# A graph network's edge stage: the transposed one-hot compared from row lists that SP loads, instead of transposed on TensorE

## The chip, the cores and the metric

The kernel runs on one core of a Trainium2 chip. The metric is the device time of one execution in microseconds (us). The profile is of one execution; its span runs from the first instruction to the last. Five engines have instruction queues of their own: TensorE (PE), VectorE (DVE), ScalarE (ACT), GpSimd (POOL) and SyncE (SP, which here only issues transfers). DMA engines move data beside them.

## The reference, cut to what matters

A message-passing layer over 3125 nodes with 103,125 edges, then a node update and a feed-forward block on half of the nodes. The edge part is the larger one:

```python
hi = h[ei]                      # h: 3125 x 256, the layer-normed nodes
hj = h[ej]
x = jnp.concatenate((hi, hj, d2), axis=-1)
msg = jax.nn.silu(x @ mW1 + mb1)
msg = _layer_norm(msg, ln_g, ln_b)
msg = jax.nn.silu(msg @ mW2 + mb2)
agg = jax.ops.segment_sum(msg, ei, num_segments=h.shape[0])
y = jnp.concatenate((h, agg), axis=-1)
y = jax.nn.silu(y @ uW1 + ub1) @ uW2 + ub2
```

`ei` is a sorted list of nodes, `ej` the other end of each edge, `d2` one weight per edge.

## The kernel before

It has three blocks of code, each ended by a barrier over the engines.

**First block (0 to 423 us).** The product with mW1 is taken once per node and not per edge: `a_sb` holds `h @ mW1[0:256]` in SBUF, 25 blocks of 125 nodes, each as a high and a low part, and in partitions 125 to 127 below the nodes the weight row of `d2`; `b_table` holds `h @ mW1[256:512] + mb1` in DRAM. The edges are grouped by block of their node `ei` into 834 tiles of 128 edges (`TILES`), and one record per edge is scattered to `rec_d` in DRAM. A record has six planes (`PLANES`): 0 is the edge's node number in its block, plus one (zero for padding), 1 to 3 the weight `d2` split in three bf16 parts, 4 and 5 the number of node `ej` as two parts. At the end of the block SP loads the records back as `recT` (tile in the partition, L261, seven groups of up to 128 tiles), PE transposes each plane (L601), and ACT and DVE copy them in turn to `rec` (edge in the partition, L365 and L759).

**Second block, the edge stage (423 to 2013 us).** Its loop runs over 417 pairs of tiles (`PAIRS`), six pairs (`RING`) to an iteration of the hardware loop; the first 3 iterations (`PEEL`) and the last are written out. The code of each engine is one `slot(t, ...)` per pair, in which each step works on an older pair: `has(t, 3)` is the step for pair t - 3. The order inside a slot is written by hand, and semaphores tie the engines. The steps of one pair, with the slot in which each stands:

- DVE, slot t: `index` computes the gather indices of pair t + 2 (L1014), POOL gathers two tiles of rows of `b_table` to `g_rows` (L862) as soon as they are there.
- DVE, slot t: `ohb`, edge by node one-hot of both tiles (L1105: bf16 compare of `iota_n` with plane 0), and a copy of the three weight parts to columns 125 to 127 (L1107).
- slot t+1: PE transposes it to `psT` (L949), ACT copies `psT` to `ohT` (L906, two buffers).
- slot t+2: PE multiplies `ohT` with the block of `a_sb`, high and low part, two tiles: `psH` (L958, four products). DVE adds `psH` to `g_rows` (L1122).
- slots t+3 to t+9: ACT's silu to `act1` (L911), DVE's statistics of the rows (L1129), a rsqrt in 16 small DVE steps per three pairs (`newton`), ACT's normalization `normed` (L899).
- slots t+10 to t+14: PE transposes to `psM` (L976), ACT copies to `nT` (L920), PE multiplies with `w2g` to `ps2` (L984), ACT's silu to `msg` (L916), DVE's float32 one-hot `ohf` (L1114), PE's product `psG` that sums the edges per node (L967), DVE's two additions to `agg` (L1023).

PE's order in a slot is psT, psH, psG, psM, ps2. DVE's is agg, agg, ohb, its copy, idx_pair, ohf, g_rows, statistics, with rsqrt steps between them in two slots of three. In this stage SP loads six weights of the next block and then all of `x` to `x_sb` (L848, L849) and has nothing else to do; POOL clears `agg` after the sixth pair's gathers (L871), and after its last gather adds `h_sb` and a bias to `x_sb` (L882, L886).

**Third block (2013 us to the end).** Node update, feed-forward, ranking and output. The change leaves it as it is.

## Time and profile before

| | |
|---|---|
| three runs | 2300.64, 2305.55 and 7235.58 us, median 2305.55 |
| the profiled execution | 2300.03 us |
| its span | 2298.3 us |
| mean granted TensorE clock | 0.947 of 2.4 GHz |
| busy in the span: PE, DVE, ACT, POOL | 88%, 87%, 60%, 45% |

A row of the profile names a group of instructions by line, engine, operation, the tensors out<-in (buffer numbers left out) and shapes. A float32 product counts as two rows. The tile `ps` is `ps2`. A length is from an instruction's start to its end; successive instructions of one engine overlap by some of it, so what an instruction costs its engine is read from start to start. "Idle before" is time in which an engine had nothing running, with what released it; "issue" stands where the profile shows no releaser. PE's ends are modelled, its starts are better.

### The profile page before, as it was taken

The numbers are of one execution on the slowest core, as the hardware profiler recorded it, in microseconds if no ns is written. First come the engines' busy times: TensorE is split into PE (matmuls) and PEld (weight loads), VectorE is DVE, ScalarE is ACT, GpSimd is POOL, SyncE is SP. The second block draws the span as 40 slices with busy tenths as digits, with TensorE's granted clock in tenths as the row PEclk, the third lists the DMA queues.
The fourth block names the chain that finished last, engine by engine and source line by source line (L and its number), as shares of the span: only waits on it lengthen the run. The fifth ranks groups of instructions, "written<-read, shape, count | busy, mean of one in ns | idle before, by whom it ended". The sixth has DMA issues, their size and how long they took to land. (4 is left out here: it accounts for less than half of the span.)

```text
span 2298.3 us, 51635 instructions
## 1 busy us (share of the span) xinstructions
PE 2029.3 (88%) x11892; PEld 1711.3 (74%) x11893; DVE 1999.2 (87%) x6778; ACT 1385.4 (60%) x2909; POOL 1035.3 (45%) x1037
## 2 busy tenths in 40 slices
PE   3555764499999999999999999999999998799996
PEld 2324553388888888888888888888888886677775
DVE  6899999599999999999999999999999999736795
ACT  1112331388888888787777777777777776423331
POOL 8752222555555555555555555555555556203000
PEclk9987776599999999999999999999999999899998
DMA  3000000432222222222222222222222222010001
GB/s 122 0 1 24 25 25 17 147 94 71 73 71 73 69 73 72 70 73 71 71 73 69 72 71 71 73 71 71 73 71 71 71 70 59 1 40 1 28 1 56
DMA packets 65908, 135.17 MB, mean 59 GB/s; under 512 B 20973, under 2 KB 36451, under 8 KB 65606
## 3 DMA queue, kind: packets, MB, share of 16 engines
q0 software_dynamic: 42016, 111.40, 17.0%
q1 hardware_dynamic: 22577, 22.31, 3.1%
q10 hardware_dynamic: 1266, 0.83, 0.2%
q8 instruction: 27, 0.44, 0.1%
q14 instruction: 22, 0.18, 0.0%
HBM read 124.33 MB, written 10.16 MB: 59 GB/s over the span
## 5 line engine op out<-in xcount | busy, mean ns | idle before, releaser
L862 POOL DMA_INDIRECT g_rows<-b_table,idx_pair x834 | 790.4, 948 | 733.0 <-DVE idx_pair L1014 591.6
L984 PE MATMUL ps<-w2g,nT 128*128 128x256 f32 x3336 | 789.1, 379 | 0.0
L984 PEld LDWEIGHTS ps<-w2g,nT 128*128 128x128 f32 x3336 | 601.5, 190 | 64.5
L899 ACT ACTIVATE normed<-act,shift,rstd_e 128x255 f32<-128x255 f32 x834 | 453.8, 596 | 196.7 <-DVE shift L1086 196.2
L1023 DVE TENSOR_TENSOR agg<-psG,agg 125x256 f32 x834 | 348.4, 418 | 121.6 <-PE psG L967 41.5
L967 PE MATMUL psG<-msg,ohf 128*125 128x256 f32 x1668 | 430.1, 380 | 0.0
L1129 DVE BATCH_NORM_STATS2 stat_e<-act 128x6 f32<-128x256 f32 x834 | 313.8, 423 | 0.0
L958 PE MATMUL psH<-a_sb,ohT 128*128 x1668 | 304.4, 305 | 0.0
L920 ACT ACTIVATE nT<-psM 128x512 f32<-128x512 f32 x417 | 249.0, 597 | 90.1 <-PE psM L976 88.9
L967 PEld LDWEIGHTS psG<-msg,ohf 128*125 128x125 f32 x1668 | 283.9, 187 | 25.1 <-ACT msg L916 0.2
L1122 DVE TENSOR_TENSOR g_rows<-psH,g_rows 128x512 f32<-128x512 f32 x417 | 289.4, 694 | 11.5 <-DMA g_rows<-b_table,idx_pair 8.5
L911 ACT ACTIVATE act<-g_rows 128x512 f32<-128x512 f32 x417 | 260.4, 624 | 8.2 <-DVE g_rows L1122 8.0
L976 PE MATMUL psM<-identf,normed 128*128 128x128 f32 x1668 | 251.2, 273 | 0.0
L916 ACT ACTIVATE msg<-ps 128x512 f32<-128x512 f32 x417 | 246.4, 591 | 5.2 <-PE ps L984 5.2
L976 PEld LDWEIGHTS psM<-identf,normed 128*128 128x128 f32 x1668 | 209.1, 142 | 43.0 <-issue 0.2
L958 PEld LDWEIGHTS psH<-a_sb,ohT 128*128 128x128 f32 x1668 | 228.0, 193 | 0.9 <-issue 0.3
L906 ACT ACTIVATE ohT<-psT 128x256 fp32r<-128x256 bf16 x417 | 157.2, 377 | 79.8 <-PE psT L949 78.7
L1105 DVE TENSOR_TENSOR ohb<-iota_n,rec 128x250 bf16<-128x250 bf16 x417 | 175.7, 421 | 0.2 <-issue 0.2
L1114 DVE TENSOR_TENSOR ohf<-iota_n,rec 128x250 f32<-128x250 bf16 x417 | 173.5, 416 | 0.0
L949 PEld LDWEIGHTS psT<-identb,ohb 128*128 128x128 bf16 x834 | 81.1, 98 | 109.4 <-DVE ohb L1107 48.5
L949 PE MATMUL psT<-identb,ohb 128*128 128x128 bf16 x834 | 116.1, 221 | 48.4 <-DVE ohb L1107 39.7
L494 POOL DMA_INDIRECT rec_d<-recw,dest x62 | 59.8, 964 | 176.2 <-ACT recw L333 91.3
(201 smaller groups left out, 2406.1 us busy)
## 6 DMA issues: line engine op xcount, KB each, us to landing
g_rows<-b_table,idx_pair POOLq DMA_INDIRECT x834
h_sb<-in_x SPq DMA_DIRECT2D x1, 3125.0 KB
b_table<-b_out SPq DMA_DIRECT2D x25, 125.0 KB
x_all<-in_x SPq DMA_DIRECT2D x1, 3125.0 KB
out<-x_all SPq DMA_DIRECT2D x5, 625.0 KB
rec_d<-rec SPq DMA_DIRECT2D x1, 1668.0 KB, 8.7
agg<-rec_d SPq DMA_DIRECT2D x6, 256.0 KB, 4.2
row<-score_d SPq DMA_DIRECT2D x1, 1525.9 KB
```

Source lines behind the costliest of these rows:

```text
L862: pool.indirect_dma_start(g_rows[:, j, n, :], None, b_table[:, :], bass.IndirectOffsetOnAxis(ap=idx_pair[:, j, n:n + 1], axis=0)).then_inc ...
L899: ins = nc.scalar.activation(normed[:, (j - 9) % 2, n, 0:D - 1], act1[:, (j - 9) % RING, n, 0:D - 1], ACT.Identity, scale=rstd_e[:, 1 - fa ...
L911: nc.scalar.activation(act1[:, (j - 3) % RING, :, :], g_rows[:, (j - 3) % RING, :, :], ACT.Silu).then_inc(s_act1, 1)
L916: nc.scalar.activation(msg[:, j % 2, :, :], ps2[:, j % 2, :, :], ACT.Silu).then_inc(s_msg, 1)
L920: nc.scalar.activation(nT[:, j % 2, :, :, :], psM[:, :, :, :], ACT.Copy).then_inc(s_nT, 1)
L958: mm = pe.matmul(psH[:, j % 2, n, :], ohT[:, j % 2, n, :], rows, start=(part == 0), stop=(part == 1))
L967: mm = pe.matmul(psG[0:NB, k, n, :], ohf[:, k, n, :], msg[:, k, n, :], start=True, stop=True)
L976: mm = pe.transpose(psM[:, n, q, :], normed[:, j % 2, n, q * P:(q + 1) * P], identf[:, :])
L984: mm = pe.matmul(ps2[:, k, n, :], nT[:, k, n, q, :], w2g[:, q, :], start=(q == 0), stop=(q == 1))
L1023: V.tensor_tensor(room, psG[0:NB, j % 2, n, :], room, ALU.add).then_inc(s_agg, 1)
L1122: V.tensor_tensor(g_rows[:, k, :, :], psH[:, j % 2, :, :], g_rows[:, k, :, :], ALU.add).then_inc(s_hid, 1)
L1129: ins = V.bn_stats(stat[:, q // 3, 2 * (q % 3) + n, :, :].rearrange("p h w -> p (h w)"), act1[:, q, n, :])
```

## The change

The transposed one-hot (node in the partition, edge in the column) is no longer made by transposing `ohb`. It is compared directly, by one DVE instruction per pair: a row list of the 256 edges' node numbers, the same in all 125 partitions, against the partition's own number (`node_col`). SP loads the lists, three pairs at a time (a half ring), from the DRAM tensor `loc_d` to `loc_rows`, broadcast to 125 partitions; and in a second transfer the three weight parts from `ew_d` into partitions 125 to 127 of `ohT`, which now has six buffers. Both DRAM tensors are written at the end of the first block from `recT`, whose tile-in-partition form has the edges of a tile in a row already: DVE copies plane 0 to `loc_c`, ACT planes 1 to 3 to `ew_c` as float32, SP stores them. Only planes 0, 4 and 5 are still transposed into `rec`, all of them copied by DVE. `ohb`, `psT` and ACT's copy are gone. The float32 one-hot `ohf` compares against a float32 row `nodes` in PSUM in place of the bf16 `iota_n` in SBUF.

```diff
@@ first block, SP: after the seven loads of recT
+                for g in range(TG):
+                    n = min(P, TILES - g * P)
+                    sp.wait_ge(s_locc, g + 1)
+                    sp.dma_start(loc_d[g * P:g * P + n, :], loc_c[0:n, g, :]).then_inc(s_rows_out, 16)
+                    sp.wait_ge(s_ewc, g + 1)
+                    sp.dma_start(ew_d[g * P:g * P + n, :, :].rearrange("t n r -> t (n r)"),
+                                 ew_c[0:n, g, :, :].rearrange("t n r -> t (n r)")).then_inc(s_rows_out, 16)
+                sp.wait_ge(s_rows_out, 32 * TG)
...
@@ first block, ACT
-                for g in range(0, TG, 2):
+                for g in range(TG):
                     n = min(P, TILES - g * P)
-                    act.wait_ge(s_rx, g + 1)
-                    nc.scalar.activation(rec[:, g * P:g * P + n, 0:PLANES], psR[:, 0, :, 0:n].rearrange("p n t -> p t n"),
-                                         ACT.Copy).then_inc(s_rec[0], 1)
+                    act.wait_ge(s_recT[g], 16)
+                    nc.scalar.activation(ew_c[0:n, g, :, :], recT[0:n, g, :, 1:4].rearrange("t r n -> t n r"),
+                                         ACT.Copy).then_inc(s_ewc, 1)
...
@@ first block, PE
-                    for k in range(PLANES):
-                        mm = pe.transpose(psR[:, g % 2, k, 0:n], recT[0:n, g, :, k], identb[0:n, 0:n])
+                    for k, plane in enumerate((0, 4, 5)):
+                        mm = pe.transpose(psR[:, g % 2, k, 0:n], recT[0:n, g, :, plane], identb[0:n, 0:n])
...
@@ first block, DVE
-                for g in range(1, TG, 2):
+                for g in range(TG):
+                    n = min(P, TILES - g * P)
+                    dve.wait_ge(s_recT[g], 16)
+                    V.tensor_copy(loc_c[0:n, g, :], recT[0:n, g, :, 0]).then_inc(s_locc, 1)
+                for g in range(TG):
                     n = min(P, TILES - g * P)
                     dve.wait_ge(s_rx, g + 1)
-                    V.tensor_copy(rec[:, g * P:g * P + n, 0:PLANES],
-                                  psR[:, 1, :, 0:n].rearrange("p n t -> p t n")).then_inc(s_rec[1], 1)
+                    V.tensor_copy(rec[:, g * P:g * P + n, 0:3],
+                                  psR[:, g % 2, :, 0:n].rearrange("p n t -> p t n")).then_inc(s_rec, 1)
...
@@ edge stage, SP
+                def body(d):
+                    for h in range(2):
+                        first = d * RING + h * (RING // 2)
+                        if not has(first, 0):
+                            continue
+                        need(sp, s_first, first - RING // 2)
+                        own = bass.ds(2 * first, RING)
+                        sp.dma_start(loc_rows[:, h, :, :].rearrange("p t e -> p (t e)"),
+                                     loc_d[own, :].rearrange("(a t) e -> a (t e)", a=1).broadcast_to([NB, RING * P])).then_inc(
+                            s_loc_in[h], 16)
+                        sp.dma_start(ohT[NB:P, h * (RING // 2):(h + 1) * (RING // 2), :, :].bitcast(F32).rearrange(
+                            "k t n e -> k (t n) e"), ew_d[own, :, :].rearrange("t k e -> k t e")).then_inc(s_ew_in[h], 16)
+
+                filling(body)
                 for to, frm in todo:
                     sp.dma_start(to, frm, allow_slow_non_contiguous=True).then_inc(s_late, 16)
                 sp.dma_start(x_sb[:, :, :], x_v).then_inc(s_xin, 16)
+                with sp.Fori(PEEL, DG) as d:
+                    body(d)
+                draining(body)
...
@@ edge stage, ACT
-                    if has(t, 1):
-                        act.wait_ge(s_turned, t)
-                        need(act, s_first, t - 2)
-                        nc.scalar.activation(ohT[:, (j - 1) % 2, :, :], psT[:, :, :],
-                                             ACT.Copy).then_inc(s_ohT, 1)
...
@@ edge stage, PE
-                    if has(t, 1):
-                        pe.wait_ge(s_oh, t)
-                        need(pe, s_ohT, t - 1)
-                        for n in range(2):
-                            mm = pe.transpose(psT[:, n, :], ohb[:, (j - 1) % RING, n, :], identb[:, :])
-                        mm.then_inc(s_turned, 1)
                     if has(t, 2):
+                        k = (j - 2) % RING
+                        if k % 3 == 0:
+                            pe.wait_ge(s_ew_in[k // 3], 16 * (d + 1 if j >= 2 else d))
                         pe.wait_ge(s_ohT, t - 1)
...
-                                mm = pe.matmul(psH[:, j % 2, n, :], ohT[:, j % 2, n, :], rows,
+                                mm = pe.matmul(psH[:, j % 2, n, :], ohT[:, k, n, :], rows,
...
@@ edge stage, DVE
-                    if has(t, 0):
-                        need(dve, s_turned, t - RING + 1)
-                        own = bass.ds(2 * t, 2)
-                        V.tensor_tensor(ohb[:, j, :, 0:NB], iota_n[:, 1:NB + 1].unsqueeze(1).broadcast_to([P, 2, NB]),
-                                        rec[:, own, 0].unsqueeze(2).broadcast_to([P, 2, NB]), ALU.is_equal)
-                        V.tensor_copy(ohb[:, j, :, NB:P], rec[:, own, 1:4]).then_inc(s_oh, 1)
+                    if has(t, 1):
+                        k = (j - 1) % RING
+                        if k % 3 == 0:
+                            dve.wait_ge(s_loc_in[k // 3], 16 * (d + 1 if j >= 1 else d))
+                        need(dve, s_first, t - RING)
+                        V.tensor_scalar(ohT[0:NB, k, :, :].rearrange("p n e -> p (n e)"), loc_rows[:, k // 3, k % 3, :],
+                                        node_col[0:NB, 0:1], None, ALU.is_equal).then_inc(s_ohT, 1)
...
-                        V.tensor_tensor(ohf[:, j % 2, :, :], iota_n[:, 1:NB + 1].unsqueeze(1).broadcast_to([P, 2, NB]),
+                        V.tensor_tensor(ohf[:, j % 2, :, :], nodes[:, :].unsqueeze(1).broadcast_to([P, 2, NB]),
```

How the instructions stand at three places. SP in the edge stage of before, from its first transfer to its last (`uw` are the next block's weights):

```order
L848 DMA uw<-in_L_gnn_uW 128x4x256
L848 DMA uw<-in_L_gnn_uW 128x2x256
L848 DMA ub1c<-in_L_gnn_ub 128x2x1
L848 DMA ub2b<-in_L_gnn_ub 128x256
L848 DMA wrb<-in_L_ffn_wr 128x256
L848 DMA brb<-in_L_ffn_br 128x1
L849 DMA x_all<-in_x 125x25x256
```

SP in the edge stage of the change, from the weights' load of the last of the six half rings that are written out to the first of the loop:

```order
L880 DMA ohT<-ew_d 3x6x128
L885 DMA uw<-in_L_gnn_uW 128x4x256
L885 DMA uw<-in_L_gnn_uW 128x2x256
L885 DMA ub1c<-in_L_gnn_ub 128x2x1
L885 DMA ub2b<-in_L_gnn_ub 128x256
L885 DMA wrb<-in_L_ffn_wr 128x256
L885 DMA brb<-in_L_ffn_br 128x1
L886 DMA x_all<-in_x 125x25x256
L887 UNCONDITIONAL_BRANCH
L887 ISA
L877 ISA [waits s_first]
L877 DMA loc_rows<-loc_d 125x768
```

The load of `x` has moved behind four waits on the loop's progress (`s_first`, before the third to the sixth half ring) and stands now in front of the loads of all later half rings.

PE inside the loop, one slot of before (ISA rows set an address register; a product of `x4` is four):

```order
L949 MATMUL psT<-identb,ohb 128x128 x2
L955 ISA
L958 MATMUL psH<-a_sb,ohT 128x256
L958 ISA
L958 MATMUL psH<-a_sb,ohT 128x256
L955 ISA
L958 MATMUL psH<-a_sb,ohT 128x256
L958 ISA
L958 MATMUL psH<-a_sb,ohT 128x256
L967 MATMUL psG<-msg,ohf 125x256 x2
L976 MATMUL psM<-identf,normed 128x128 x4
L984 MATMUL ps<-w2g,nT 128x256 x4
```

and one slot of the change:

```order
L987 ISA
L990 MATMUL psH<-a_sb,ohT 128x256
L990 ISA
L990 MATMUL psH<-a_sb,ohT 128x256
L987 ISA
L990 MATMUL psH<-a_sb,ohT 128x256
L990 ISA
L990 MATMUL psH<-a_sb,ohT 128x256
L999 MATMUL psG<-msg,ohf 125x256 x2
L1008 MATMUL psM<-identf,normed 128x128 x4
L1016 MATMUL ps<-w2g,nT 128x256 x4
```

The two transposes are gone and nothing else has moved, so psH follows ps2 of the slot before it directly.

DVE inside the loop, from the second agg addition of a slot, before:

```order
L1023 TENSOR_TENSOR agg<-psG,agg 125x256
L1040 TENSOR_TENSOR tmp<-stat_e 128x6
L821 REGISTER_ALU
L1105 ISA [waits s_turned]
L1105 TENSOR_TENSOR ohb<-iota_n,rec 128x2x125
L1107 ISA
L1107 COPY ohb<-rec 128x2x3
L1042 TENSOR_TENSOR tmp<-stat_e 128x6
```

and in the change, in a slot that begins a half ring:

```order
L1055 TENSOR_TENSOR agg<-psG,agg 125x256
L1072 TENSOR_TENSOR tmp<-stat_e 128x6
L1137 ISA
L843 REGISTER_ALU [waits s_loc_in0]
L1139 TENSOR_SCALAR ohT<-loc_rows,node_col 125x256 [waits s_first]
L1074 TENSOR_TENSOR tmp<-stat_e 128x6
```

One instruction stands where two stood. Before it wrote the one-hot of pair t, for PE's next slot; now it writes that of pair t - 1, also for PE's next slot.

## Rows read from the trace of the kernel before

**Rows 1.** the page, section 1: busy time, share of the span, instructions, by engine

```profile
PE 2029.3 (88%) x11892; PEld 1711.3 (74%) x11893; DVE 1999.2 (87%) x6778; ACT 1385.4 (60%) x2909; POOL 1035.3 (45%) x1037
```

**Rows 2.** stretches, mid-loop: length, busy us and instructions by engine, granted clock, DMA share, GB/s

```profile
600.00:1900.00 1300.00, 1300.00 (x7795) 1137.10 (x7794) 1196.61 (x5069) 1020.10 (x2126) 670.31 (x708) 1.00 0.25 71
```

**Rows 3.** PE in order of time, one slot: start us, length us, engine, line, operation, count

```profile
1200.27 0.27 PE L949 MATMUL psT<-identb,ohb 128*128 128x128 bf16 x2
...
1202.20 1.89 PE L984 MATMUL ps<-w2g,nT 128*128 128x256 f32 x8
...
1203.93 0.28 PE L949 MATMUL psT<-identb,ohb 128*128 128x128 bf16 x2
...
1204.02 0.71 PE L958 MATMUL psH<-a_sb,ohT 128*128 x4
...
1204.57 1.03 PE L967 MATMUL psG<-msg,ohf 128*125 128x256 f32 x4
```

**Rows 4.** DVE in order of time, mid-loop; in brackets idle before it and its releaser

```profile
1200.39 0.41 DVE L1023 TENSOR_TENSOR agg<-psG,agg 125x256 f32 x1
...
1204.15 0.41 DVE L1023 TENSOR_TENSOR agg<-psG,agg 125x256 f32 x1
...
1205.12 0.41 DVE L1105 TENSOR_TENSOR ohb<-iota_n,rec 128x250 bf16<-128x250 bf16 x1
1205.45 0.17 DVE L1107 COPY ohb<-rec 128x6 bf16 x1
1205.52 0.15 DVE L1069 TENSOR_TENSOR tmp<-tmp 128x6 f32<-128x6 f32 x1
...
1209.03 0.99 DVE L1023 TENSOR_TENSOR agg<-psG,agg 125x256 f32 x2 [1.06 <-issue]
```

**Rows 5.** PE in order of time, in the drain

```profile
1976.19 1.03 PE L967 MATMUL psG<-msg,ohf 128*125 128x256 f32 x4
...
1979.04 0.82 PE L958 MATMUL psH<-a_sb,ohT 128*128 x4
1979.69 1.03 PE L967 MATMUL psG<-msg,ohf 128*125 128x256 f32 x4
...
1982.72 1.03 PE L967 MATMUL psG<-msg,ohf 128*125 128x256 f32 x4
```

**Rows 6.** groups by line before 440 us: shapes, count, busy us and mean ns, idle

```profile
L749 DVE TENSOR_SCALAR w2g<-w2raw,gcol 128x256 f32<-128x256 f32 x2 | 0.6, 344 | 0.0
```

**Rows 7.** SP's issues in order of time: start us, length us, DMA, count

```profile
2.54 0.32 SPq L243 DMA_DIRECT2D h_sb<-in_x  x1
2.90 25.96 SPq L244 DMA_DIRECT2D wij<-in_L_gnn_mW  x1
...
426.45 0.34 SPq L849 DMA_DIRECT2D x_all<-in_x  x1
```

**Rows 8.** stretches, while h_sb is loaded; columns as in rows 2

```profile
12.00:16.00 4.00, 0.00 (x0) 0.00 (x0) 3.78 (x9) 0.00 (x0) 0.48 (x1) 1.00 0.34 121
```

**Rows 9.** DMA issues: queue, operation, count, KB each, median us to landing

```profile
rec_d<-rec SPq DMA_DIRECT2D x1, 1668.0 KB, 8.7
...
wrb<-in_L_ffn_wr SPq DMA_DIRECT2D x1, 128.0 KB, 4.9
```

**Rows 10.** waits of SP's queue: line, waited for, us in total, times, longest

```profile
SPq L851 <- DMA x_all<-in_x: 41.5, 1, 41.5
```

**Rows 11.** PE in order of time, after the idle time in the drain

```profile
1970.00 0.39 PE L949 MATMUL psT<-identb,ohb 128*128 128x128 bf16 x2 [27.68 <-DVE ohb L1107]
...
1971.23 1.91 PE L967 MATMUL psG<-msg,ohf 128*125 128x256 f32 x4
```

**Rows 12.** all engines in order of time, around the start of the edge stage

```profile
413.47 3.15 SPq L261 DMA_DIRECT2D agg<-rec_d  x7
...
433.51 0.69 DVE L1122 TENSOR_TENSOR g_rows<-psH,g_rows 128x512 f32<-128x512 f32 x1 [8.31 <-DMA g_rows<-b_table,idx_pair]
```

**Rows 13.** one line of the kernel, L1107: ns min/median/max, first and last start

```profile
L1107 DVE COPY ohb<-rec x417: 157/165/5952, 424.0 to 1973.4; 128x6 bf16 x132, 128x6 bf16<-128x6 bf16 x7
```

More of the change, by code:

```diff
@@ L94, in build @@
         rec = alloc(edge_mem, "rec", [P, TILES + 2 * LEAD, 8], BF16)
+        node_col = alloc(edge_mem, "node_col", [P, 1], F32)
         tile_block = alloc(edge_mem, "tile_block", [1, TG * P], I32)
@@ L228, in build @@
             s_rx = sem("s_rx")
-            s_rec = [sem("s_rec0"), sem("s_rec1")]
+            s_locc = sem("s_locc")
+            s_ewc = sem("s_ewc")
+            s_rows_out = sem("s_rows_out")
+            s_rec = sem("s_rec")
             s_tb = sem("s_tb")
@@ L769, in build @@
             idx_pair = sb("idx_pair", [P, RING, 2], I32)
-            ohb = sb("ohb", [P, RING, 2, P], BF16)
-            ohT = sb("ohT", [P, 2, 2, P], F32R)
+            loc_rows = sb("loc_rows", [NB, 2, RING // 2, 2 * P], BF16)
+            ohT = sb("ohT", [P, RING, 2, P], F32R)
             ohf = sb("ohf", [P, 2, 2, NB], F32)
@@ L781, in build @@
             shift = sb("shift", [P, 2, 6], F32)
-            psT = ctx.enter_context(nc.psum_tensor("psT", [P, 2, P], BF16))
+            nodes = ctx.enter_context(nc.psum_tensor("nodes", [P, NB], F32))
             psH = ctx.enter_context(nc.psum_tensor("psH", [P, 2, 2, D], F32))
@@ L794, in build @@
             s_gather = [sem(f"s_gather{j}") for j in range(RING)]
-            s_ohw = sem("s_ohw")
-            s_oh = sem("s_oh")
-            s_turned = sem("s_turned")
+            s_loc_in = [sem("s_loc_in0"), sem("s_loc_in1")]
+            s_ew_in = [sem("s_ew_in0"), sem("s_ew_in1")]
+            s_nodes = sem("s_nodes")
             s_ohT = sem("s_ohT")
@@ L990, in body @@
                     for j in range(RING):
-                        slot(d * RING + j, j)
+                        slot(d * RING + j, d, j)
                 filling(body)
@@ L1013, in index @@
                     own = bass.ds(2 * t, 2)
-                    V.scalar_tensor_tensor(out=idx_pair[:, j, :], in0=rec[:, own, 4], scalar=64.0, in1=rec[:, own, 5],
+                    V.scalar_tensor_tensor(out=idx_pair[:, j, :], in0=rec[:, own, 1], scalar=64.0, in1=rec[:, own, 2],
                                            op0=ALU.mult, op1=ALU.add).then_inc(s_idx, 1)
@@ L1140, in _ @@
                     index(t, t)
+                V.tensor_copy(nodes[:, :], iota_n[:, 1:NB + 1]).then_inc(s_nodes, 1)
+                dve.wait_ge(s_nodes, 1)
                 filling(body)
```

12 lines of the change are left out of this document (9 added, 3 removed).

## The prediction

> **What bounds the kernel now.** I read the page's first section first: TensorE (PE) is busy 88% of the span and VectorE (DVE) 87%, ScalarE (ACT) 60%, GpSimd (POOL) 45% [rows 1]. Two engines that close need the stage itself. The table of stretches shows from 600 to 1900 us, inside the edge loop, PE busy for all 1300 of 1300 us at a granted clock of 1.00 (2.4 GHz), DVE for 1197 and the DMA engines for a quarter [rows 2]. So I read one slot of the loop (one pair of tiles) in order of time on PE: the first psT product starts at 1200.27 and the next slot's at 1203.93, so a slot is 3.66 us [rows 3]. The loop from 456 to 1940 us holds about (1940 - 456) / 3.67 = 404 such full slots of the 417; the others are filling and draining.
>
> Does DVE bind as well? Its slots begin with an agg addition: two slots with rsqrt steps in them take some 3.76 us each (1200.39 to 1204.15), and before the third DVE stands idle for 1.06 us [rows 4]. So it needs about 3.67 - 1.06 / 3 = 3.32 us per slot. It has 0.35 us of slack, and PE sets the pace. POOL issues two gathers a slot and has about half of the slot free.
>
> **The change, part by part.**
>
> *PE loses the two transposes into psT (404 slots).* In a full slot psT starts 0.09 us before psH (1203.93 to 1204.02) and psH 0.55 us before psG, together 0.64 us [rows 3]. The smaller bound is therefore 0.09 us a slot. The larger one stands in the drain: exactly one slot there has psH and no psT. Its psG follows the previous psG after 1979.69 - 1976.19 = 3.50 us; the next slot, with neither, takes 1982.72 - 1979.69 = 3.03 us [rows 5]. So psH alone costs 0.47 us and psT plus psH 0.64: without psT a slot is 3.50 us, 0.17 less. That psH gets cheaper too is plausible, since its first weight load then stands behind a 0.21 us ps product (eight from 1202.20 to 1203.93) instead of behind a short transpose. I take 3.50, since it is the very sequence of the changed kernel at full clock, though it is one slot only. Gain: 404 x 0.17 = 69 us; with 0.09 it is 36.
>
> *ACT loses the copy of psT to ohT.* It is not the bound; nothing.
>
> *DVE loses ohb and its 6-column copy, and gains one tensor_scalar of 125x256 from bf16 in SBUF to ohT.* Start to start the old two take 0.33 + 0.07 = 0.40 us [rows 4]. The trace has no such operation on bf16; the nearest is w2g, 128x256 with a scalar per partition, 344 ns [rows 6]. The old pieces of 250 columns last 412 ns and cost 0.33, so the new one costs 0.27 to 0.33. DVE goes from 3.32 to about 3.2 us, under 3.50. The ohf compare reads its node numbers from PSUM now; agg, which reads PSUM too, lasts 0.41 us as ohb does [rows 4], so nothing. If PE's cover were gone DVE would still be 0.07 to 0.13 us quicker than before.
>
> *The order of the dependences.* Pair t is compared in DVE's slot t+1 and multiplied in PE's slot t+2, as the ACT copy was. DVE's compare lies early in a slot, two thirds of a slot or more ahead of the next psH. Its new waits: s_loc_in every third slot, and s_first of six pairs ago, which is long past. PE's new one is s_ew_in every third slot. Behind a late s_loc_in stands all of DVE's slot: the next index (so the gathers), the g_rows addition and the statistics.
>
> *SP loads 139 half rings of lists*, 125 partitions x 1536 bytes (188 KB) plus 9 KB of weights, each when the third pair before it is multiplied: that is 3 slots plus about one us before DVE needs it, some 11 us. Bounds of its time: h_sb, also 125 partitions, moved 3125 KB from 2.54 us to 28.86 at 121 GB/s, at which 188 KB take 1.6 us plus the fixed part [rows 7, 8]; the 128-partition broadcast wrb, 128 KB, landed in 4.9 us beside other loads [rows 9]. So 3.5 to 7 us against 11: hidden. The traffic is 188 KB per 10.5 us, 18 GB/s beside 71 for the gathers.
> The Trainium skill (DMA: Bandwidth & Descriptors, section "Why a DMA increments its semaphore by 16 and not by 1") says that the slowest dimension picks how many of the 16 engines a transfer uses, 5 for 125 partitions. The trace agrees: h_sb alone kept a share of 0.34 busy [rows 8].
>
> *SP's order moves the load of x (3125 KB).* It was issued at 426.45, at the head of the stage [rows 7], and no engine but SP waited for it until the loop's end. Now it stands behind six half rings and six weight loads, and in front of the list for pair 18. The sixth half ring (pairs 15 to 17) is let go when pair 11 is multiplied (PE slot 13); eight issues at about 0.45 us later, slot 14, x starts. DVE needs pair 18's list in slot 19, five slots or 18.5 us later. How long is x? 26.4 us nearly alone (h_sb) [rows 7], 41.5 us in the place it had, beside gathers (SP's own wait for it) [rows 10]. And does the list wait for it? The issue behind h_sb stood 25.96 us on SP, until h_sb was through [rows 7]; so yes. With x at 33 us, between the two because DVE's stall stops the gathers, plus 4.9 for the list: a stall of 33 + 4.9 - 18.5 = 19 us, bounds 13 and 28, and zero if the list's packets went beside x. After it PE restarts at the half clock: the slot after the idle 27.68 us in the drain has its psG at 1.91 us instead of 1.03 [rows 5, 11], so 2 us more. Sum +21, once.
>
> *Before the stage:* 14 more stores by SP behind the seven loads that took 3.15 us to issue, so 6.3 us of issues, overlapped with copies; 1.5 MB to store at the rate of rec_d (1668 KB in 8.7 us) is 8 us [rows 9, 12], starting as the first list lands. The rec copies now are all DVE's, seven of half the size. Most of it lies beside the transposes that ended the block before, so +3 us (0 to 8).
>
> *The stage's start:* the first gather was waited for until 433.51, 8.31 us, while x and the weights came in [rows 12]. Now only lists compete: -2 us (-4 to 0). POOL's clearing of agg blocks DVE as before, and POOL's additions to x after the last gather too.
>
> **Sum**, against the profiled execution (2300.03 us; the median of the runs shown, 2305.55, is 5 above): 2300 - 69 + 21 + 3 - 2 = 2253; I say 2255.
>
> **Rivals.**
> *A, the forecast: PE-bound at 3.50, x stalls the loop once.* 2255, own range 2235 to 2275. Chance 0.50, a little over half of it more than 2% under 2305.55 (below 2259).
> *B, no stall by x:* 2300 - 69 + 1 = 2232. For it: interleaving can't be ruled out, since h_sb's successor was a different transfer in a fuller queue. 0.12.
> *C, psT was worth only its 0.09 us:* 2300 - 36 + 22 = 2286. For it: only one slot shows 3.50. 0.14.
> *D, DVE's new operation meets GpSimd.* A copy of ohb stood 5.95 us while POOL cleared agg, and its median beside 50% gathers is 165 ns against a minimum of 157 [rows 13]. So gathers don't hold that 6-column copy. If they held the wider operation, it would meet one half of the time and wait half of 0.95 us, 0.25 us: DVE at 3.45 to 3.5, where every jitter shows; I price it at 3.58 a slot, 2300 - 36 + 22 = 2286 up to 2310. 0.10. The Trainium skill (SBUF — State Buffer, section "SBUF: two separate sides", its trap on DVE blocking DMA) says that a two-port DVE operation keeps GpSimd from writing descriptors; that would delay a gather by the operation's 0.3 us, out of a half-free slot.
> *E, slower: the lists come late each half ring.* It decides once a list needs more than the 11 us between its release and DVE's slot. Each us beyond that costs 139 us; at 13 us the kernel takes 2255 + 278 = 2530. Against it: 4.9 us for wrb. For it: the list's source is read 125 times from one row of DRAM, and no row shows that beside gathers. 0.08.
> Unnamed, anywhere: 0.06.
>
> About 2% is what a measurement of this kernel can tell from no change. Faster by over that: 0.28 of A, B, a little unnamed: 0.42. Slower: E, 0.02 of D, 0.02 unnamed: 0.12. Within: 0.46. The range goes from B to D's middle: 2228 to 2298.
>
> **What would show it.** PE's psG to psG in mid-loop: 3.50 (A, B), 3.58 (C, D). DVE's idle before agg: still about 0.9 us per three slots if PE leads, gone if D. One stall of 13 to 28 us on DVE near pair 18, some 490 us into the span, ended by the load of loc_rows, and x landing just before; none means B. DVE's waits for loc_rows each third slot mean E. The mean of the new tensor_scalar: 0.28 to 0.42 us long; more means D. First instruction of the edge stage at 425 to 431 us instead of 423.5. I am wrong if mid-loop slots are over 3.6 us, or if stall and prologue together exceed 35 us.

## The result and the profile after

The changed kernel takes 2271.84 us (median of four runs, 2270.75 to 2273.65), where the kernel before took 2304.62 in the same session (median of four, one of which took 7235.58). The ratio, which leaves that one run out, is 0.9865, with a 95% interval of 0.9848 to 0.9882. That is 1.35% faster, inside the 2% that I called "no change", 17 us above the 2255 I forecast and inside the range of 2228 to 2298. The profiled execution has a span of 2268.9 us against 2298.3. Its first section, to be read beside [rows 1]:

```profile
PE 1973.4 (87%) x11037; PEld 1678.5 (74%) x11038; DVE 1948.0 (86%) x6373; ACT 1295.1 (57%) x2495; POOL 1035.7 (46%) x1038
```

PE has 855 instructions fewer (834 of them the transposes into psT), DVE 405, ACT 414. A bare look at the shares says that nothing changed: two engines at 87% and 86%, as before. So I lined the two traces up by one event that both have, the start of DVE's addition `g_rows += psH` for pair p:

| pair | before, us | after, us | difference | what lies in between |
|---|---|---|---|---|
| 0 | 433.51 | 435.26 | +1.8 | prologue, first list, first gather |
| 15 | 478.98 | 482.20 | +3.2 | filling |
| 17 | 486.55 | 511.93 | +25.4 | the stall behind x: +22.2 |
| 30 | 534.54 | 558.32 | +23.8 | |
| 400 | 1894.32 | 1869.44 | -24.9 | 370 slots: -48.7, 3.675 to 3.544 us a slot |
| 416 | 1980.10 | 1953.54 | -26.6 | drain |
| end of span | 2298.3 | 2268.9 | -29.4 | the next block: -2.8 |

The last 2.8 us lie in a block that the change does not touch. PE's first row in it stands at 2013.2 us before and at 1986.9 after. Its first 15 us before, then after (columns as in [rows 2]; the clock is the third figure from the end), and PE's first 32 psU products in each:

```profile
2013.00:2028.00 15.00, 13.83 (x52) 9.92 (x53) 0.00 (x0) 4.42 (x8) 0.54 (x3) 0.77 0.49 150
2017.87 10.53 PE L1329 MATMUL psU<-fT,uw 128*128 128x320 f32 x32 [0.68 <-ACT fT L1270]
```

```profile
1986.64:2001.64 15.00, 13.38 (x68) 9.80 (x68) 0.00 (x0) 6.13 (x12) 0.54 (x3) 1.00 0.50 149
1990.83 8.68 PE L1364 MATMUL psU<-fT,uw 128*128 128x320 f32 x32 [0.68 <-ACT fT L1305]
```

The same 32 products take 10.53 us at a mean granted clock of 0.77 and 8.68 at 1.00; that is most of the 2.8 us, and luck as far as the change goes. From pair 416 to the end of the span the fourteen traces vary by 5.9 us (312.6 to 318.5).

The stall, on SP's queue and then on DVE, in order of time (start us, length us; in brackets the idle time before and what ended it):

```profile
467.84 0.26 SPq L877 DMA_DIRECT2D loc_rows<-loc_d  x1
...
472.76 0.37 SPq L886 DMA_DIRECT2D x_all<-in_x  x1
478.50 25.27 SPq L877 DMA_DIRECT2D loc_rows<-loc_d  x1
503.96 0.26 SPq L880 DMA_DIRECT2D ohT<-ew_d  x1
...
510.71 0.35 DVE L1139 TENSOR_SCALAR ohT<-loc_rows,node_col 125x256 fp32r<-125x256 bf16 x1 [22.34 <-DMA loc_rows<-loc_d]
```

The first issue behind x stands 25.27 us on SP. DVE waits 22.34 us for that list, and every engine is idle with it, as the stretches of the changed kernel show (columns as in [rows 2]):

```profile
500.00:510.00 10.00, 0.00 (x0) 0.00 (x0) 0.00 (x0) 0.00 (x0) 0.00 (x0) 0.50 0.34 121
510.00:520.00 10.00, 8.72 (x41) 7.68 (x41) 8.93 (x37) 4.43 (x9) 4.58 (x5) 0.76 0.21 63
600.00:1900.00 1300.00, 1300.00 (x7340) 1151.09 (x7339) 1191.07 (x4893) 976.01 (x1833) 695.84 (x734) 1.00 0.34 93
```

x moves at 121 GB/s with a DMA share of 0.34, the very figures of h_sb [rows 8]. By the Trainium skill (DMA: Bandwidth & Descriptors, section "Why a DMA increments its semaphore by 16 and not by 1") 125 partitions use 5 of 16 engines, a share of 0.31; the trace agrees, here as for h_sb. In mid-loop the DMA share is 0.34 instead of 0.25 and the traffic 93 GB/s instead of 71 [rows 2]: the lists are there, and nothing waits for them.

Now the slot. PE's psG products in mid-loop:

```profile
1203.99 1.03 PE L999 MATMUL psG<-msg,ohf 128*125 128x256 f32 x4
...
1207.49 1.02 PE L999 MATMUL psG<-msg,ohf 128*125 128x256 f32 x4
...
1211.11 1.12 PE L999 MATMUL psG<-msg,ohf 128*125 128x256 f32 x4
...
1214.71 1.02 PE L999 MATMUL psG<-msg,ohf 128*125 128x256 f32 x4
...
1218.21 1.03 PE L999 MATMUL psG<-msg,ohf 128*125 128x256 f32 x4
```

The distances between them are 3.50, 3.62, 3.60 and 3.50 us. Four of the six slots of a pass take the forecast's 3.50, two take 3.6, and the pass 21.26 us instead of 21.0. DVE in the same pass, in order of time:

```profile
1205.05 0.35 DVE L1139 TENSOR_SCALAR ohT<-loc_rows,node_col 125x256 fp32r<-125x256 bf16 x1
1205.31 0.16 DVE L1101 TENSOR_TENSOR tmp<-tmp 128x6 f32<-128x6 f32 x1
1205.42 0.16 DVE L1046 SCALAR_TENSOR_TENSOR idx_pair<-rec 128x2 int32 x1
...
1207.61 0.15 DVE L1118 SCALAR_TENSOR_TENSOR shift<-tmp,rstd_e 128x6 f32<-128x6 f32 x1
1208.86 0.99 DVE L1055 TENSOR_TENSOR agg<-psG,agg 125x256 f32 x2 [1.10 <-PE psG L999]
```

The new operation costs 0.26 us from start to start, just under the 0.27 to 0.33 that I had put. The 1.10 us of idle time is the point. The profile names PE's psG as its end, but psG of 1203.99 had long been done. In it stands work of DVE's own sequencer at the end of a pass of the loop: a branch and the load of twelve block numbers into registers. In the changed kernel, the times of that load (ns min/median/max, first and last start us):

```profile
L1042 DVEq TENSOR_LOAD <-tile_block x2: 851/851/851, 1207.6 to 1228.9; - x2
```

It comes every 21.3 us, once in six slots. In the kernel before the same load took 848 ns and began at 1207.8, inside the 1.06 us of [rows 4]. That branch and load fill the idle time is read from their place and length; no run took them out. What every trace shows is the 1.1 us itself, once a pass. The Trainium skill (DMA: Bandwidth & Descriptors, section "Latency and other measured facts") gives a floor of about 600 ns for such a load; here twelve registers took 851.

### The profile page after: what moved, and what is told of

Its sections match the earlier page's. It is cut to its first block and busy times, and to the rows that moved or that the text cites. A ratio compares the mean times of both kernels' runs of the same rounds, so it can differ in the third digit from the quotient of the medians.

```text
span 2268.9 us, 48446 instructions
## 1 busy us (share of the span) xinstructions
PE 1973.4 (87%) x11037; PEld 1678.5 (74%) x11038; DVE 1948.0 (86%) x6373; ACT 1295.1 (57%) x2495; POOL 1035.7 (46%) x1038
## 5 line engine op out<-in xcount | busy, mean ns | idle before, releaser
L999 PE MATMUL psG<-msg,ohf 128*125 128x256 f32 x1668 | 435.4, 383 | 0.0
L990 PE MATMUL psH<-a_sb,ohT 128*128 x1668 | 344.2, 329 | 67.6 <-issue 47.8
L990 PEld LDWEIGHTS psH<-a_sb,ohT 128*128 128x128 f32 x1668 | 258.6, 192 | 97.4 <-issue 76.1
L951 ACT ACTIVATE msg<-ps 128x512 f32<-128x512 f32 x417 | 241.5, 579 | 5.2 <-PE ps L1016 5.2
L1147 DVE TENSOR_TENSOR ohf<-nodes,rec 128x250 f32<-128x250 f32 x417 | 173.4, 416 | 0.0
L1139 DVE TENSOR_SCALAR ohT<-loc_rows,node_col 125x256 fp32r<-125x256 bf16 x417 | 150.3, 361 | 26.4 <-DMA loc_rows<-loc_d 26.1
L594 PE MATMUL psK<-oqv,or_ 128*128 128x96 bf16 x806 | 55.7, 232 | 80.6 <-DVE oqv L741 80.6
L349 ACT ACTIVATE recw<-psK 128x96 bf16<-128x96 f32 x62 | 15.4, 250 | 178.4 <-PE psK L594 151.8
L732 DVE TENSOR_TENSOR or_<-x_all,psV 128x1664 bf16<-128x1664 f32 x62 | 116.4, 1877 | 0.0
```

The source lines that it names most:

```text
L951: nc.scalar.activation(msg[:, j % 2, :, :], ps2[:, j % 2, :, :], ACT.Silu).then_inc(s_msg, 1)
L990: mm = pe.matmul(psH[:, j % 2, n, :], ohT[:, k, n, :], rows, start=(part == 0), stop=(part == 1))
L999: mm = pe.matmul(psG[0:NB, k, n, :], ohf[:, k, n, :], msg[:, k, n, :], start=True, stop=True)
```

## The experiments

Experiments 1 to 4 ran in one session, in which the kernel before took 2301.12 us. In the two sessions after it, it took 2316.37 and 2317.37, and in the last 2300.45. I call the first and the last calm and the two between them disturbed. It isn't the chip: one chip gave 2301, 2317 and 2300. Ratios are to the kernel before in the same session, and they do not take the session out: the same kernel has 0.9805 in a disturbed session and 0.9703 in a calm one (experiment 8), some 23 us apart. So times of experiments 5 to 7, all from disturbed sessions, are set against the changed kernel only to about that much; lengths in their traces are used where they can be.

What is different shows in the traces in mid-loop (600 to 1900 us). The disturbed ones have waits of ACT and DVE whose releaser the profile gives as "remote", together 48 to 347 us, and the calm ones have none. The same kernel in a disturbed session (engine and line, waited for, us in total, times, longest):

```profile
ACT msg L954 <- remote: 100.9, 78, 4.9
ACT nT L958 <- remote: 88.2, 35, 3.1
```

These waits come with loop passes of 24 to 26 us among normal ones, and the pipeline fills later (pair 15 at 489.8 us or later instead of 482 to 483).

**1. x in 25 pieces.** Is the stall the lists' place behind x?

```diff
-                sp.dma_start(x_sb[:, :, :], x_v).then_inc(s_xin, 16)
-                with sp.Fori(PEEL, DG) as d:
+                with sp.Fori(PEEL, PEEL + BLOCKS) as d:
+                    body(d)
+                    one = bass.ds(d - PEEL, 1)
+                    sp.dma_start(x_sb[:, one, :], x_v[:, one, :]).then_inc(s_xin, 16)
+                with sp.Fori(PEEL + BLOCKS, DG) as d:
                     body(d)
...
```

> The changed kernel with the one load of x taken apart: 25 pieces of 125 KB, one in each of the first 25 passes of SP's loop, behind the lists of that pass. Theory (the stall at 478 to 511 us is the lists standing behind x's 3.2 MB on one queue): at 121 GB/s a piece takes 1.1 us, which the 10.5 us between two half rings hide; the waits of SP (25.27 us) and of DVE (22.34 us) go, the clock does not fall to 0.5, and the time falls by 20 to 25 us, to 2247 to 2252, with a mid-loop slot of 3.54 as before. Rival 1 (the bandwidth that x takes, whatever its order, holds up lists and gathers): the same wait comes in pieces, most of the 20 us stays, 2262 to 2272. Rival 2 (the missing 17 us of the forecast came from x too, by a lasting effect on the pipeline's phase): the slot also falls to 3.50, 2230 to 2235.

Measured: 2248.43 us (ratio 0.9767, 0.9750 to 0.9783), 23.4 less than the changed kernel (22.6 by the ratios). Pair 17 starts at 490.42 instead of 511.93, and the mid-loop slot is 3.541 us: the first theory, and neither rival. SP's issues in order of time:

```profile
490.26 0.26 SPq L877 DMA_DIRECT2D loc_rows<-loc_d  x1
490.71 0.26 SPq L880 DMA_DIRECT2D ohT<-ew_d  x1
491.20 0.28 SPq L889 DMA_DIRECT2D x_all<-in_x  x1
500.75 0.26 SPq L877 DMA_DIRECT2D loc_rows<-loc_d  x1
```

No issue stands. The load of x costs nothing that the slot shows (3.541 against 3.544) when its pieces lie between two lists.

**2. x issued by ACT.** Order in one queue, or bandwidth?

```diff
+                        if isinstance(d, int) and d * RING + j == 13:
+                            act.dma_start(x_sb[:, :, :], x_v).then_inc(s_xin, 16)
```

> The changed kernel with the whole load of x issued by ACT at about the same time (behind ACT's slot 13, some 470 us) instead of by SP. Theory A (first in, first out: the lists wait only because they stand in SP's queue behind x): SP's wait at the list load goes, DVE's longest wait is under 3 us, and the time falls by 18 to 25 us, to 2247 to 2254. Theory B (the 16 DMA engines are shared, and x's traffic slows whatever else is loaded): the lists and the gathers land late for as long as x is moving, a stall of 10 us or more stays (at 187.5 KB a half ring, half the bandwidth would still bring a list in 3 us, so B needs more than fair sharing), 2260 to 2272.

Measured: 2249.36 us (0.9775, 0.9758 to 0.9791). The transfer is the same, whole and 2.6 us earlier, on another queue. ACT's queue and SP's in order of time, then the stretch:

```profile
470.17 0.29 ACTq L960 DMA_DIRECT2D x_all<-in_x  x1
...
479.51 0.30 SPq L877 DMA_DIRECT2D loc_rows<-loc_d  x1
```

```profile
500.00:510.00 10.00, 10.00 (x60) 8.92 (x58) 8.53 (x33) 7.64 (x15) 4.77 (x6) 1.00 0.50 165
```

The list's issue takes 0.30 us instead of 25.27 and the engines work on while 165 GB/s move. So the 22 us were the order in SP's queue, and the bandwidth of x was harmless.

**3. No compare for the second one-hot.** Who sets 3.544? The kernel leaves out DVE's compare in the loop, so its sums are not the reference's.

```diff
-                    if has(t, 12):
-                        V.tensor_tensor(ohf[:, j % 2, :, :], nodes[:, :]..., rec[:, ..., 0]..., ALU.is_equal).then_inc(s_ohf, 1)
```

> The changed kernel without DVE's compare for the second one-hot (ohf, 416 ns by its rows, some 0.33 us from start to start, once a slot): ohf is filled twice ahead of the loop and left, so the sums by node are not the reference's. PE's work is unchanged. Theory (DVE sets the slot in the changed kernel: 6 x 3.36 + 1.1 us at its loop's end = 21.26 us a pass, where PE needs 21.0): DVE's pass falls to 19.3 us, PE's 3.50 decides, the slot falls from 3.544 to 3.50, and the time by 15 to 19 us, to 2253 to 2257. Rival (PE's own loop end costs the 0.26 us a pass): slot 3.54, time within 3 us of 2272.

Measured: 2247.21 us (0.9768, 0.9752 to 0.9784), 24.6 less. The slot is 3.497 us, and all 62 mid-loop passes take 20.97 to 20.99. DVE is busy 1111 of 1300 us and now waits for PE's psH, which it does not in the changed kernel. The stretch, and the wait (engine and line, waited for, us in total, times, longest):

```profile
600.00:1900.00 1300.00, 1297.97 (x7424) 1161.45 (x7422) 1111.25 (x4562) 998.39 (x1857) 705.64 (x743) 1.00 0.34 94
```

```profile
DVE g_rows L1152 <- PE psH L990: 59.5, 146, 0.7
```

The two spans differ by 23.2 us: 17.1 lie in the 370 slots, as the theory has it; another 2.5 in pairs 17 to 30, 0.8 in the drain and 2.8 in the next block, which the edit doesn't touch. The expectation had counted the slots alone.

**4. The same cut in the kernel before.**

> The same cut in the kernel before: the compare that writes ohf is made twice ahead of the loop and left, so the sums by node are not the reference's. DVE's pass there is 22.05 us, PE's 22.0. Theory (PE set the slot before, DVE stood just under it): the slot stays 3.667 to 3.675, and the time falls by 0 to 4 us, 2300 to 2305. Rival (DVE set the slot before as well, and PE's rows of 3.667 are only DVE's pace): the slot falls by 0.02 us or more, the time by 8 us or more, to 2296 or less.

Measured: 2298.18 us (0.9986, 0.9976 to 0.9996), 2.9 less. PE in order of time:

```profile
1200.78 1.02 PE L968 MATMUL psG<-msg,ohf 128*125 128x256 f32 x4
1203.81 0.28 PE L949 MATMUL psT<-identb,ohb 128*128 128x128 bf16 x2
1204.44 1.02 PE L968 MATMUL psG<-msg,ohf 128*125 128x256 f32 x4
```

Every pass takes 22.00 us, against 22.05 in the kernel before. DVE waits for psH now, 177 times in mid-loop, so 22.00 us is what PE needs; the kernel before, in which DVE never waits for psH, takes the 22.05 that DVE needs. The two bounds lay 0.05 us apart. Experiments 3 and 4 take the same work from DVE; it is worth 17 us in the loop where PE needs 21.0, and 3 where it needs 22.0.

**5. Two transposes back on PE, of a constant, without a wait.** Their PSUM tile takes the place of `nodes`, so ohf compares against the bf16 row in SBUF again (417 ns; 416 in the kernel before).

```diff
+                        for n in range(2):
+                            pe.transpose(psT[:, n, :], iota_n[:, :], identb[:, :])
...
```

> The changed kernel with two transposes of 128x128 BF16 put back on PE in every slot, of a constant, into a PSUM tile that nobody reads and without a wait; the second one-hot is compared from the constant in SBUF again, as in the kernel before (416 ns either way by the rows). So DVE keeps its relief and PE loses its own. Theory (the two transposes cost PE 0.17 us a slot, and PE at 3.667 decides again): slot 3.66 to 3.68 against 3.544, 404 slots by 0.124 = +50 us, 2318 to 2326. Rival (the transposes slip into gaps of PE, and what the change gained was DVE's work and the round trip of the psT copy on ACT): slot under 3.60, 2272 to 2290.

Measured: ratio 1.0062 (1.0045 to 1.0079), 2330.31 us; by its ratio the changed kernel would take 0.9865 x 2316.37 = 2285 there, so +45, give or take what the session does. The trace doesn't depend on that. PE in order of time:

```profile
762.59 1.03 PE L1001 MATMUL psG<-msg,ohf 128*125 128x256 f32 x4
...
765.62 0.28 PE L982 MATMUL psT<-identb,iota_n 128*128 128x128 bf16 x2
...
766.26 1.03 PE L1001 MATMUL psG<-msg,ohf 128*125 128x256 f32 x4
```

psG follows psG after 3.66 or 3.67 us nearly everywhere in mid-loop, and the mean slot is 3.678. The transposes are worth 0.17 us of PE's slot, as the forecast had it, without any round trip through ACT. With them back, DVE's relief brings nothing, and what is left is the stall.

The trace also shows what DVE needs by itself. At 648.5 us a long pass had put 7.4 us between two g_rows of DVE, where 3.67 is normal; while DVE catches up, its passes are 21.31 and 21.25 us long and PE's 22.00. DVE, one row a pass, then PE:

```profile
677.20 0.69 DVE L1157 TENSOR_TENSOR g_rows<-psH,g_rows 128x512 f32<-128x512 f32 x1
...
698.51 0.69 DVE L1157 TENSOR_TENSOR g_rows<-psH,g_rows 128x512 f32<-128x512 f32 x1
...
719.76 0.68 DVE L1157 TENSOR_TENSOR g_rows<-psH,g_rows 128x512 f32<-128x512 f32 x1
```

```profile
678.26 1.03 PE L1001 MATMUL psG<-msg,ohf 128*125 128x256 f32 x4
...
700.26 1.03 PE L1001 MATMUL psG<-msg,ohf 128*125 128x256 f32 x4
```

DVE's own pass with the change is thus 21.25 us, the mid-loop pass of the changed kernel.

**6. Lists let go two pairs later.**

```diff
-                        need(sp, s_first, first - RING // 2)
+                        need(sp, s_first, first - RING // 2 + 2)
```

> The changed kernel with each half ring of lists released two pairs later (SP waits for psH of pair first-2 instead of first-4): the release then comes about 2.5 us ahead of the compare that needs the list, and the first list of the stage took 4.4 us from its issue (428.11) to the compare (432.54). Theory (lists are harmless only because of their lead, and every us that they are late costs once a half ring, since DVE sets the slot): late by 1.5 to 2.5 us in each of 139 half rings, +200 to +330 us, 2480 to 2600. Rival (in mid-loop a list lands in 2.5 us or less, or PE's lead takes it up): under +60 us.

Measured: 2305.40 us, ratio 0.9951 (0.9935 to 0.9967), 20 us above the changed kernel by ratio, which is within what the session alone can do, and far from the 200 and more that I expected. DVE waited for lists in mid-loop four times, together 4.4 us:

```profile
DVE ohT L1139 <- DMA loc_rows<-loc_d: 4.4, 4, 1.2
```

54 of 62 mid-loop passes take 21.2 to 21.4 us, as with the early lists. The extra is 9 us in the filling (pair 15 at 491.15 instead of 482.20) and five passes that last 24.4 to 26.1. Both belong to the session: the other kernels of the disturbed sessions have pair 15 at 489.8 to 495.7, with the lists let go early. So the later lists cost the 4.4 us of waits and nothing more that can be seen. My expectation took the landing time of the very first list, 4.4 us, for that of all. The forecast's rival E (lists late in every half ring) has about two slots of room: let go that much later, the lists only begin to be waited for.

**7. The indices off DVE.** If DVE sets the slot, taking its index operation away should bring PE's 3.50. All indices are made once, and ACT copies two a slot:

```diff
+                def index(t, j):
+                    nc.scalar.activation(idx_pair[:, j, :], idx_all[:, bass.ds(2 * t, 2)], ACT.Copy).then_inc(s_idx, 1)
...
+                    if has(t, 0):
+                        index(t + LEAD, (j + LEAD) % RING)
```

> The changed kernel with DVE's index operation (two elements, once a slot, about 0.1 us from start to start) taken from its loop: all indices are made in one DVE operation ahead of the loop, and ACT, which has idle time, copies two of them a slot into the ring. Theory (DVE sets the slot by 21.26 us a pass, PE needs 21.0): DVE's pass falls by some 0.5 us, PE's 3.50 decides, the slot falls from 3.544 to 3.50 and the time by 14 to 22 us, to 2250 to 2258, less 1 to 2 for the big operation. Rival 1 (ACT's new 0.2 us a slot lengthens its chain of waits to psM and normed): slot 3.54 or more. Rival 2 (the 24.6 us of the run without ohf came from its lighter load on PSUM or from the filling, not from DVE's share of the slot): under 10 us.

> Both edits on the changed kernel: x in 25 pieces, one a pass, and the indices copied by ACT. The two causes lie in different places (the stall at 478 to 511 us, the slot from 530 us on), so theory says that they add: 23.4 + 14 to 22 us, 2226 to 2235. Rival (the stall hid part of the filling's cost or the index copies on ACT eat the rest): 2238 or more, one of the two gains lost.

Measured: 2563.04 us, ratio 1.1048 (1.1026 to 1.1070), and with x split 2538.20, 1.0935 (1.0905 to 1.0965). The slot is 4.27 us. The x split kept its 25 us. The index edit went with some 280 us by the ratio, in a disturbed session; it was never run in a calm one. Two more kernels, both with x split, went after that. One has DVE make the indices of three pairs in one operation, once in three slots; one has ACT's copy at the head of its slot, about 1.8 us earlier:

> The changed kernel with x in 25 pieces and DVE's index operation made once in three slots for three pairs (6 elements), behind g_rows of the slot two ahead of the first of them, instead of once a slot for one. DVE's work falls by two operations of 0.08 to 0.1 us in three slots. Theory (DVE sets the slot, the gathers have lead enough): DVE's pass falls to under 21.0, PE's 21.0 decides, slot 3.50, 68 by 0.26 = -17 us, ratio to before 0.969 to 0.972. Rival (what made the kernel with ACT's index copies 10% slower is the gathers' release, three pairs in a bunch, and not ACT): here too POOL issues three pairs in a row after a wait, DVE waits for gathers in mid-loop, slot 3.6 to 4.3, ratio 0.99 to 1.09.

> The changed kernel with x in 25 pieces and the index copies on ACT, but at the head of ACT's slot, ahead of the two normed operations, instead of behind act1 (there the slot was 4.26 us). The index is then ready about 1.8 us earlier, ACT's work is the same. Theory A (the late release of the gathers was what cost 0.7 us a slot): the slot falls to 3.50 to 3.60, ratio to before 0.97 to 0.98. Theory B (the small operation on ACT itself disturbs: ACT's own chain to msg and nT, or something of that chip): slot 4.2 or more as before, ratio over 1.08.

Measured: 2591.73 us, ratio 1.1182 (1.1159 to 1.1205), slot 4.39, with ACT not involved; and 2314.17, ratio 0.9984 (0.9974 to 0.9994), slot 3.68, with ACT's copy early. So ACT's small operation is not needed for the loss. What the three slow ones share is that POOL waits up to 5 or 7 us for indices and then issues its gathers without a pause. From the kernel with three pairs at a time, POOL, then PE and ACT, in order of time:

```profile
1205.36 0.95 POOL L905 DMA_INDIRECT g_rows<-b_table,idx_pair  x1 [4.68 <-DVE idx_pair L1048]
1206.61 0.94 POOL L905 DMA_INDIRECT g_rows<-b_table,idx_pair  x1 [0.30 <-issue]
...
1211.62 0.95 POOL L905 DMA_INDIRECT g_rows<-b_table,idx_pair  x1 [0.30 <-issue]
```

```profile
1208.06 0.60 PE L1011 MATMUL psM<-identf,normed 128*128 128x128 f32 x4
...
1212.58 0.60 ACT L958 ACTIVATE nT<-psM 128x512 f32<-128x512 f32 x1 [5.01 <-remote]
```

Six gathers stand from 1205.36 to 1212.57. PE's psM ends at 1208.66, ACT's copy of it starts only at 1212.58, and DVE's next g_rows, for a psH that ended at 1210.85, at 1214.34. By counting the rows, the gather that this g_rows needs belongs to the bunch before, whose last issue was at 1199.74; in the three slow kernels every gather in mid-loop is issued 10.4 us or more before the g_rows that needs it, and in the changed kernel 9.9 or more. So the gathers are not late. Nor is a row of six enough: the six closest starts of a pass span 7.6 us in the changed kernel and 7.3, at one place 6.4, in experiment 3 (calm), and no pass of either is long; in the slow kernels it is 6.7 and 6.3. The rival is the session: all four kernels with changed indices ran in disturbed sessions, and the "remote" waits that end ACT's and DVE's idle time here are in every trace of those sessions and in no calm one. The session alone is not enough either: experiments 5 and 6 have slots of 3.68 and 3.60 us in it. Whether the index edits cost anything in a calm session is untested, and why ACT and DVE start 3.5 us or more after the PE rows that they need is open.

**8. One small DVE operation less.** This way to relieve DVE leaves the indices and gathers alone. The sum of the means and the sum of the moments become one operation over 12 elements, on top of the split x:

```diff
-                        V.tensor_tensor(mean2, m0, m1, ALU.add).then_inc(s_newton, 1)
...
-                        V.tensor_tensor(moment, q0, q1, ALU.add).then_inc(s_newton, 1)
+                        V.tensor_tensor(tmp[:, 1:3, :].rearrange("p w k -> p k w"), stat[:, par, :, 0, 1:3],
+                                        stat[:, par, :, 1, 1:3], ALU.add).then_inc(s_newton, 1)
...
```

> The changed kernel with x in 25 pieces (as before: 2248 where the kernel before took 2301, ratio 0.977) and one DVE operation less in each three slots: the sum of the two halves' means and the sum of their moments are made by one operation over 12 elements instead of two over 6. Theory (DVE sets the slot; its pass of 21.26 us falls by twice 0.08 us): pass 21.10, slot 3.517, 68 passes by 0.16 = -11 us, ratio to before 0.972 to 0.974. Rival 1 (what DVE saves is lost in its waits, or PE's loop end is the bound): pass 21.25, ratio 0.976 to 0.978. Rival 2 (the 12-element operation is slower by what is saved): the same.

> The same kernel as in the run of the merged sum (x in 25 pieces, one DVE operation less in three slots) once more. There, 50 or so of its 62 mid-loop passes took 21.0 to 21.4 us, and nine took 22.9 to 24.9, with ACT and DVE idle for 2 to 5 us behind PE's rows; the kernel before was itself 0.7% slower in that session than where the split was measured. Theory 1 (the long passes belong to the session, not to the kernel): where the kernel before takes 2301 us again, the long passes are gone, slot 3.51 to 3.52, 2236 to 2242, ratio 0.972 to 0.974; where it takes 2317 again, they are there again, ratio 0.980. Theory 2 (the faster DVE itself brings the long passes): they are there whatever the kernel before takes, ratio 0.979 to 0.982.

Measured first, in a session with the kernel before at 2317: ratio 0.9805 (0.9781 to 0.9829), 54 of 62 mid-loop passes at 21.0 to 21.44, seven of 22.9 to 24.9 (the nine of my expectation were a miscount). Measured again, with the kernel before at 2300: 2232.67 us, ratio 0.9703 (0.9690 to 0.9716), no long pass, slot 3.502. So the long passes belonged to the session, and they cost this kernel 41 us (2273.87 against 2232.67) where the kernel before lost 17. PE and DVE in order of time in the second run:

```profile
1202.67 1.03 PE L1002 MATMUL psG<-msg,ohf 128*125 128x256 f32 x4
...
1206.17 1.02 PE L1002 MATMUL psG<-msg,ohf 128*125 128x256 f32 x4
```

```profile
1203.46 0.17 DVE L1075 TENSOR_TENSOR tmp<-stat_e 128x12 f32<-128x12 f32 x1
```

The pass is 21.01 us, within 0.03 of what PE needs (20.99 in experiment 3). I had allowed 0.16 us for the two operations saved in a pass; 21.26 became 21.01, so they were worth 0.25. Why more is not shown. The rsqrt steps' starts lie 0.07 us before the next operation in some places and up to 0.22 in others. This kernel beats both: 3% under the kernel before, 1.6% under the changed one.

## Why the prediction was right or wrong

*PE's 0.17 us from the transposes: right.* It rested on one slot of the drain, which was indeed the sequence of the changed kernel: 3.50 in four of six slots (after), in all of them once DVE is out of the way (experiments 3 and 8), and 3.67 again with the transposes back (experiment 5). Rival C (0.09 us, 3.58 a slot) is out.

*"Before the third slot DVE stands idle for 1.06 us. So it needs 3.32 us per slot. It has 0.35 us of slack": wrong, and this is the step that failed.* The idle time was read once, in a window of 9 us, and spread over three slots. It comes once in six, and it is no slack: DVE has it in every pass, also when it lags behind PE, where its sequencer branches and loads registers. DVE needed 22.05 us a pass, that is 3.675 a slot, not 3.32. The trace of the kernel before could have told. These are all of DVE's waits of 600 to 1900 us in it:

```profile
DVE agg L1023 <- issue: 33.7, 32, 1.1
DVE agg L1023 <- PE psG L967: 28.5, 27, 1.1
```

Both are that one gap, 59 times in 59 passes. For psH, which it would wait for if PE led, DVE never waits. The sign that I had named, idle time before agg if PE leads, cannot tell the two: the gap of 1.1 us stands once a pass whoever leads (59 times in experiment 4, where PE does). With the right number the forecast's own prices give the result: DVE trades 0.33 + 0.07 for 0.27, 0.13 us a slot or 0.80 a pass, and 22.05 - 0.80 = 21.25 is above PE's 21.0. 404 slots by 0.133 are 54 us instead of 69, and 2300 - 54 + 21 + 3 - 2 = 2268, against 2270.75 us of the profiled execution and 2271.84 of the median. This one term is 15 of the 17 us.

*The stall, +21: right in place, cause and size.* Pairs 15 to 17 lost 22.2 us, DVE waited 22.34 until 510.71, and the issue behind x stood 25.27. By pair 30 the changed kernel is 21.5 us behind experiment 1, which has no stall. The parts were each off by 2 to 3 us and partly cancel: x held the queue for 31.0 us (33 expected), the list took 6.9 more (4.9), and DVE needed it 15.6 us after x started (18.5). The reading that an issue behind a long load stands until it is through, taken from h_sb [rows 7], held, and experiment 2 shows that it holds for one queue only. Rival B is out; it had the right time only for a kernel without the stall (experiment 1: 2248, and 2232 with DVE relieved too).

*The prologue, +3 (0 to 8), and the start, -2:* SP's first issue of the edge stage came at 428.11 instead of 423.50, 4.6 us later, inside the bounds, and pair 0 came 1.8 us later where +1 was expected. Right.

*DVE's new operation: right.* 346 ns long in mid-loop, within 0.28 to 0.42, and 0.26 us from start to start. Rival D did not happen: the operation is not lengthened in mid-loop, where half the time a gather is being issued. Only in POOL's clearing of agg (444.07 to 449.53) did one last longer, 5.82 us, as the copy before did [rows 13].

*Rival E, late lists: out* (experiment 6).

*The verdict.* The forecast lay 4 us on the faster side of the 2% line at 2259, the result 13 us on the other. The largest single chance, 0.46 for "within", had that side. Of A's own range of 2235 to 2275, the result lies at the top end, because both bounds of the slot, 0.09 and 0.17 us, were PE's; DVE's was missing from them. That the time still fell into the range is partly luck: A said that PE leads, DVE does, and its need happens to lie only 0.04 us a slot above PE's. Nothing in the prediction bounded that distance.

## What to carry to other kernels

Before an engine is given slack, its need has to be taken over a whole pass of the loop. Idle time that comes once in every pass, and whose releaser is missing or had long been done, counts as work. Where two engines are both near 87%, take the pass length of each, since relief for one is worth only the distance to the other (here 0.05 us a pass before the change, 0.26 after it, with the leader the same). A long load put in a queue ahead of small loads in a loop can stop the loop for most of its length (22 of 31 us here); the same bytes on another queue, or in pieces between the small ones, were free.

## What the runs showed of the hardware that was not expected

A list of 188 KB in mid-loop lands nearly in time even if it is let go two slots later than in the changed kernel (four waits, 4.4 us together), though the first one took 4.4 us until DVE could start (428.11 to 432.54).

POOL pauses for 2.0 us between two gathers every 52 pairs (before pairs 56, 108, 160, 212, 264, 316 and 368) in thirteen of the fourteen traces, calm and disturbed, and in the kernel before too. In the calm ones no pass is longer for it. In the disturbed ones of experiments 5, 6 and 8, at the same times as five of these pauses, DVE takes 5.7 to 7.4 us from one g_rows to the next instead of about 3.5: at pairs 53 or 54, 157 or 158, 209 or 210, 313 or 314, and 365 or 366. What the pause is stays open.

Between sessions the same kernel differs by 0.7% (2300 and 2317 us for the kernel before) or by 1.8% (2232.67 and 2273.87 for the kernel of experiment 8). So a ratio to a common kernel does not carry from one session to another. Three of the kernels that move the index took 9 to 12% more than the kernel before and the fourth as much, where 2 to 3% less was expected; all four are from disturbed sessions only.
